# The opening of an attention and mixture-of-experts layer: the first tile's halves and product in front of the second tile's statistics and the weight scaling

## The chip, the cores and the metric

The kernel runs on one core of one Trainium2 chip. The metric is the device time of one execution in microseconds (us), the median of several runs. Five engines work beside each other, each through its own list of instructions in order: TensorE (PE, with its weight loads PEld), VectorE (DVE), ScalarE (ACT), GpSimd (POOL) and SyncE (SP), which here only issues DMAs. They meet by semaphores.

## The reference

The layer takes x of 8 x 512 x 256 in float32 and computes

```
x = x + attention(layernorm(x))          # q, k, v products of 256x256, causal softmax, scores / 16
x = x + ffn(layernorm(x))                # shared expert + 8 routed experts, 2 of them per token
ffn: down(silu(x gate) * (x up)), I = 512, weights of the two best sigmoid(router logits), normalised
layernorm(x) = (x - mean) / sqrt(var + 1e-5)
```

Queries and keys come in only as x Wq Wk^T x^T, so the kernel multiplies Wq and Wk^T once (wm) and needs one product t = x wm instead of two.

## The kernel before, in words

Everything that TensorE multiplies is split into two float16 parts, a high half (ScalarE copies the float32 value into float16) and a low half (the float32 value less the high half, in float16), and each product is three matmuls: high by high, high by low, low by high. So each operand passes ScalarE (names ending in `_high`) and then VectorE or GpSimd (`_low`).

The work is tiled by batch: eight tiles of 512 tokens, tile b in four blocks of 128 tokens. For each tile: statistics on VectorE (`stats_1`, line 1498, `aggregate_1`, whose last instruction writes ve, line 1490), the power -0.5 on GpSimd (`rstd1`, line 706), the shift on VectorE (`shift_1`, line 1509, writes nmr), the normalised tile on ScalarE (`xn_normalise`, line 962), its high half on ScalarE (`xn_high`, 975) and low half on GpSimd (`xn_low`, 712), a transposing DMA on SyncE's queue (`xn_transpose`, 386), then on TensorE the products t and v (`t_product`, 2333, `v_product`, 2353), their high halves on ScalarE (`t_high`, 1009, `v_high`, 1019) and low halves on VectorE (`t_low`, 1690, `v_low`, 1700), the scores, the row maxima, exp, the transposed probabilities and their product with v.

Tile 0 goes another way, so that it need not wait for a DMA: TensorE transposes it with an identity matrix (`first_transposes`, 2222), ScalarE and VectorE take the halves from PSUM (`first_xn_high`, 1087, `first_xn_low`, 1540). Two of its four blocks are normalised on VectorE.

The weights of the experts come in 36 pieces through two buffers: a load, `w_scale` (945) and `w_high` (951) on ScalarE, `w_low` (730) on GpSimd, which frees the buffer for the load two pieces on. wm, wv and the router's matrix are split at the start (`wm_low`, `wv_low`, `router_low`).

The order of the work is written out by hand: each engine has one list of calls, and an instruction whose semaphore isn't there holds back all that stands behind it on its engine. GpSimd's list begins rstd1(0), rstd1(1), the zeroing of the rows in DRAM (a DMA that it issues), rstd1(2), xn_low(1), w_low(0), put_idx(0), w_low(1), xn_low(2) (lines 785 to 793). Four waits matter near the change: `t_product(0)` waits for both low halves of tile 0 and for wm_low, `v_product(0)` for wv_low too, `t_high(0, ...)` for wv_low, whose source lies in the tensor that t_high writes, and `shift_1(2)` for rstd1(2) and for tile 1 to be normalised.

Of the kernel before, what the change touches and what calls it, by code (L numbers as in the profile page):

```python
# [91 lines left out]
def wait(eng, sem, value):  # L92

    if isinstance(value, int) and value <= 0:
        return
    eng.wait_ge(sem, value)
# [22 lines left out]
def build(nc, x, wq_t, wk_t, wv, w_all, router, bias, out):  # L119
    with ExitStack() as ctx:  # L120
# [212 lines left out]
        def bank3(o):  # L333
            return o[:, :].rearrange("p (n r) -> p n r", r=P)
# [22 lines left out]
        def blk(t3):  # L357
            return t3.rearrange("p (n d) -> p n d", n=NB)

        def w_ap(j, part, off, n):  # L360
            at_ = part * WJ + off
            if isinstance(j, int):
                return w[:, j * (2 * WJ) + at_:j * (2 * WJ) + at_ + n]
            return w[:, :].bitcast(U8)[:, ds(j * (4 * WJ) + 2 * at_, 2 * n)].bitcast(F16)
# [574 lines left out]
        def _(act):  # L939
            a = nc.scalar  # L940

            def copy(o, i, scale=1.0):
                return a.activation(o, i, ACT.Copy, scale=scale)  # L943

            def w_scale(g):

                piece = wst[:, (g % 2) * CH:(g % 2 + 1) * CH]
                act.wait_ge(w_in[g % 2], 16 * (g // 2 + 1))
                copy(piece, piece, WS).then_inc(w_scaled, 1)

            def w_high(g):

                j, c = divmod(g, CHUNKS)
                act.wait_ge(w_scaled, g + 1)
                if g == E * CHUNKS:
                    act.wait_ge(gu_mm, 4 * (B - 3) + 4)
                    act.wait_ge(xn2_lo, 2 * B - 2)
                    act.wait_ge(pt_in[1], 16 * B)
                    act.wait_ge(ln1, B * LN_STEPS)
                copy(w_ap(j, 0, c * CH, CH), wst[:, (g % 2) * CH:(g % 2 + 1) * CH]).then_inc(w_hi, 1)  # L960

            def xn_normalise(b):

                if b >= B:
                    return
                act.wait_ge(shift1, b + 1)
                if b == 1:
                    act.wait_ge(xn0_mm, 2)
                wait(act, xn_lo, b - 1)
                for i in range(2 if b == 0 else NB):  # L970
                    ins = a.activation(xn32[:, i * D:(i + 1) * D], x1[:, ds(b * (NB * D) + i * D, D)],
                                       ACT.Identity, scale=rstd[0][:, i:i + 1], bias=nmr[:, i:i + 1])
                ins.then_inc(xn_put, 1)

            def xn_high(b):

                if b >= B:
                    return
                act.wait_ge(xn_put, b + 1)
                wait(act, xnt_in, 16 * b - 16)  # L980
                copy(xnrow[:, :].rearrange("p (n c) -> p n c", n=NB)[:, :, 0:D], blk(xn32[:, :])).then_inc(xn_hi, 1)
# [27 lines left out]
            def t_high(b, m):  # L1009

                if b >= B:
                    return
                act.wait_ge(t_mm, b * KD + (m + 1))
                if b == 0:
                    act.wait_ge(wv_lo, 1)
                wait(act, s_mm, b * NB)
                copy(tt[:, m * S:(m + 1) * S], T_BANK[m][:, :]).then_inc(t_hi, 1)

            def v_high(b, m):

                if b >= B:
                    return
                act.wait_ge(v_mm, 2 * b + m + 1)
                wait(act, pv_mm, 2 * b)
                copy(v[:, m * S:(m + 1) * S], V_BANK[m][:, :]).then_inc(v_hi, 1)
# [61 lines left out]
            def first_xn_high(k):  # L1087

                act.wait_ge(xn0_mm, 2)
                copy(xnt4[:, :, k, :], bank3(XN_BANK[k])).then_inc(xn0_hi, 1)  # L1090
# [6 lines left out]
            def router_high():  # L1097

                act.wait_ge(small_in, 32)
                copy(rw[:, 0:KD * E], tt[:, 1024:1024 + 2 * KD * E].bitcast(F32), WS).then_inc(rw_hi, 1)  # L1100
# [7 lines left out]
            wv_high()  # L1108
            wm_high()
            router_high()  # L1110
            w_scale(0)
            first_xn_high(1)
            first_xn_high(0)
            xn_normalise(1)
            w_scale(1)
            xn_high(1)
            w_high(0)
            t_high(0, 0)
            w_high(1)
            t_high(0, 1)  # L1120
            v_high(0, 0)
            xn_normalise(2)
            exp_of(0, 0)
# [336 lines left out]
        def _(dve):  # L1460
# [6 lines left out]
            def low(o, full, hi, scale=None):  # L1467

                if scale is None:
                    return d.tensor_tensor(o, full, hi, ALU.subtract)  # L1470
                return d.scalar_tensor_tensor(out=o, in0=full, scalar=scale, in1=hi, op0=ALU.mult, op1=ALU.subtract)
# [4 lines left out]
            def stats_of(b, lns, tile):  # L1476

                for n in range(NB):
                    ins = d.bn_stats(tile[:, 6 * n:6 * n + 6], x_of(b)(n))
                ins.then_inc(lns, 1)  # L1480

            def aggregate(b, i, lns, shifted, tile):

                done = b * LN_STEPS
                dve.wait_ge(lns, done + 1)
                wait(dve, shifted, b)
                for n in range(NB):
                    d.bn_aggr(mv[i][:, 2 * n:2 * n + 2], tile[:, 6 * n:6 * n + 6]).then_inc(lns, 1)
                dve.wait_ge(lns, done + 5)
                d.tensor_scalar(ve[i][:, :], mv[i][:, :].rearrange("p (n c) -> p n c", c=2)[:, :, 1],  # L1490
                                EPS, None, ALU.add).then_inc(lns, 1)
# [6 lines left out]
            def stats_1(b):  # L1498

                if b < B:  # L1500
                    dve.wait_ge(x_in[b], 16)
                    stats_of(b, ln1, stats1)

            def aggregate_1(b):

                if b < B:
                    aggregate(b, 0, ln1, shift1, stats1)
# [32 lines left out]
            def first_xn_low(k):  # L1540

                dve.wait_ge(xn0_hi, k + 1)
                low(xnt4[:, :, KD + k, :], bank3(XN_BANK[k]), xnt4[:, :, k, :]).then_inc(xn0_lo, 1)

            def wv_low():

                dve.wait_ge(wv_hi, 1)
                low(wvs[:, KD * D:2 * KD * D], tt[:, 0:1024].bitcast(F32), wvs[:, 0:KD * D], WS).then_inc(wv_lo, 1)

            def router_low():  # L1550

                dve.wait_ge(rw_hi, 1)
                low(rw[:, KD * E:2 * KD * E], tt[:, 1024:1024 + 2 * KD * E].bitcast(F32), rw[:, 0:KD * E],
                    WS).then_inc(rw_lo, 1)

            def wm_low():

                dve.wait_ge(wm_hi, 1)
                low(wm[:, KD * D:2 * KD * D], PT0[:, :], wm[:, 0:KD * D], WS).then_inc(wm_lo, 1)
# [294 lines left out]
            first_xn_normalise()  # L1854
            stats_1(1)
            aggregate_1(1)
            stats_1(2)
            wm_low()
            shift_1(1)
            first_xn_low(1)  # L1860
            first_xn_low(0)
            router_low()
            aggregate_1(2)
            wv_low()
            stats_1(3)
            shift_1(2)
            t_low(0, 0)
# [902 lines left out]
```

## Time and profile before

| | |
|---|---|
| median of 3 runs | 556.28 us (555.76 to 557.24) |
| span of the profiled execution, first to last instruction | 555.3 us |
| median less that span | 0.98 us |
| PE busy | 518.0 us, 93% |
| DVE busy | 369.8 us, 67% |
| ACT busy | 301.0 us, 54% |
| POOL busy | 288.9 us, 52% |

No time beside its span is given for the profiled execution itself; the difference to the median is what this table shows. A row of a timeline has the start in us from the span's start, the length in us, the engine, the line of the kernel (a helper's line may stand for many calls), the operation, what it writes and reads with the shapes, and in brackets how long the engine was idle before and what ended that. Lengths of neighbours overlap by some 0.1 us.

### The profile page before, as it was taken

To read this page: it belongs to the slowest core of one execution; us is meant where nothing else is said; L and a number is where in the kernel's file an instruction comes from. 1 tells how busy PE (TensorE), PEld (TensorE's weight loads), DVE (VectorE), ACT (ScalarE), POOL (GpSimd) and SP (SyncE) were. 2 spreads that over 40 slices of the span, in tenths; PEclk is the share of its full clock that TensorE was granted. 3 is DMA by queue.
4 is the path that set the end of the run, shared out by engine and by line. 5 is a ranking of instruction groups with operands and counts; after the bars stand their busy time and mean duration, and the time that the engine had idled before them with its cause. 6 is when DMAs were issued, how large, how long until landed. Compare 5 with 4: busy or idle time off the path is not lost.

```text
span 555.3 us, 14903 instructions
## 1 busy us (share of the span) xinstructions
PE 518.0 (93%) x4757; PEld 425.5 (77%) x4757; DVE 369.8 (67%) x980; ACT 301.0 (54%) x580; POOL 288.9 (52%) x242
## 2 busy tenths in 40 slices
PE   4889988999999999997999999999999999999992
PEld 3557766788878888886767788888787888888881
DVE  5788998689887878899747555445454454454551
ACT  3989877678777676744233443433343433434341
POOL 4466677668676765857022344452444434434443
PEclk9999999899999999998899999999999999999998
DMA  8799848949694947414465965764846536345443
GB/s 271 201 181 208 178 127 158 217 133 209 161 208 141 194 127 170 155 70 136 131 115 85 98 107 69 103 83 60 108 59 89 73 60 97 55 65 78 62 58 38
DMA packets 139351, 68.55 MB, mean 123 GB/s; under 512 B 114608, under 2 KB 132336, under 8 KB 139280
## 3 DMA queue, kind: packets, MB, share of 16 engines
q1 hardware_dynamic: 126128, 48.84, 43.5%
q0 software_dynamic: 13152, 18.76, 19.4%
q8 instruction: 44, 0.72, 0.5%
q14 instruction: 27, 0.22, 0.1%
HBM read 19.46 MB, written 23.08 MB: 77 GB/s over the span
## 4 chain that ended last, share of the span: by engine, by line
PE 65%; DVE 12%; DMA 8%; SPq 5%; ACT 5%; issue 3%; POOL 1%; POOLq 0%; ACTq 0%; DVEq 0%
PE bank L2216 29%; PE bank L2240 15%; PE bank L2547 4%; PE bank L2322 3%; PE bank L2564 3%; DMA v<-xnrow 2%; PE bank L2625 2%; PE bank L2347 2%; PE bank L2392 2%; DMA xn2t<-xrow 2%; PE bank L2369 2%; PE bank L2640 2%; SPq L405 2%; DMA x<-x 1%; DVE h L1470 1%
## 5 line engine op out<-in xcount | busy, mean ns | idle before, releaser
L2216 PE MATMUL bank<-xn2t,w 128*128 128x256 f16 x1608 | 184.9, 273 | 1.3 <-DVE th L1653 1.1
L2216 PEld LDWEIGHTS bank<-xn2t,w 128*128 (+1 forms) x1608 | 155.2, 98 | 24.3 <-DVE th L1653 2.2
L1644 DVE SCALAR_TENSOR_TENSOR th<-th,bank 128x512 f32<-128x512 f32 x83 | 56.6, 682 | 55.2 <-ACT th L989 54.1
L2240 PE MATMUL bank<-w,h 128*128 (+1 forms) x768 | 91.5, 273 | 0.0
L943 ACT ACTIVATE h<-th 128x512 f16<-128x512 f32 (+1 forms) x69 | 42.9, 622 | 84.6 <-DVE th L1653 78.3
L989 ACT ACTIVATE th<-bank 128x512 f32<-128x512 f32 x83 | 49.2, 593 | 62.1 <-PE bank L2216 47.6
L2240 PEld LDWEIGHTS bank<-w,h 128*128 128x128 f16 x768 | 74.0, 98 | 10.4 <-DVE x L1676 0.3
L866 POOL DMA_INDIRECT out<-p,wm x28 | 43.9, 1569 | 67.2 <-ACT p L1323 27.3
L1470 DVE TENSOR_TENSOR h<-th,h 128x512 f16<-128x512 f32 (+1 forms) x69 | 50.6, 733 | 38.3 <-ACT h L943 38.1
L734 POOL TENSOR_TENSOR w<-wst,w 128x768 f16<-128x768 f32 x36 | 59.1, 1645 | 18.9 <-ACT w L943 18.7
L758 POOL DMA_INDIRECT rows<-xrow,sidx x56 | 56.5, 1009 | 17.0 <-issue 13.3
L866 POOL DMA_INDIRECT out<-phl,wm x24 | 38.1, 1587 | 39.1 <-DMA out<-tt,wm 13.0
L1653 DVE SCALAR_TENSOR_TENSOR th<-th,bank 128x512 f32<-128x512 f32 x83 | 56.8, 684 | 2.0
L866 POOL DMA_INDIRECT out<-tt,wm x12 | 19.7, 1644 | 41.0 <-DMA out<-x 17.2
L2216 PE MATMUL bank<-w 128*128 128x256 f16 x288 | 34.5, 280 | 0.0
L2547 PE MATMUL bank<-w,ptr 128*128 x144 | 33.0, 379 | 0.4 <-DMA ptr<-rows 0.4
L943 ACT ACTIVATE xnrow<-xn 128x512 f16<-128x512 f32 (+2 forms) x26 | 17.8, 684 | 26.1 <-DVE xn L2107 17.4
L2216 PEld LDWEIGHTS bank<-w 128*128 128x128 f16 x288 | 28.4, 100 | 4.2
L2322 PE MATMUL bank<-v,ptr 128*128 128x256 f16 x240 | 29.7, 273 | 1.2 <-DMA ptr<-phl 1.0
L943 ACT ACTIVATE wst<-wst 128x768 f32<-128x768 f32 x36 | 30.1, 836 | 0.6 <-DMA wst<-w_all 0.6
L943 ACT ACTIVATE w<-wst 128x768 f16<-128x768 f32 x36 | 30.1, 840 | 0.5
L704 POOL TENSOR_TENSOR rstd<-ve,halves 128x4 f32<-128x4 f32 x16 | 16.9, 1058 | 25.5 <-DVE ve L1490 23.0
(188 smaller groups left out, 808.4 us busy)
## 6 DMA issues: line engine op xcount, KB each, us to landing
wst<-w_all SPq DMA_DIRECT2D x36, 384.0 KB
x<-x SPq DMA_DIRECT2D x8, 512.0 KB, 5.6
out<-x SPq DMA_DIRECT2D x8, 512.0 KB, 4.0
rows<-xrow POOLq DMA_DIRECT2D x1, 1192.5 KB, 6.6
rows<-xrow,sidx POOLq DMA_INDIRECT x56
out<-p,wm POOLq DMA_INDIRECT x28
xn2t<-rows SPq DMA_TRANSPOSE x26
wm<-rows SPq DMA_DIRECT2D x26, 9.0 KB, 2.4
```

The costliest lines, as they stand in the source:

```text
L734: cc.tensor_tensor(w_ap(j, 1, c * CH, CH), wst[:, (g % 2) * CH:(g % 2 + 1) * CH], w_ap(j, 0, c * CH, CH), ALU.subtract).then_inc(w_lo, 1)
L758: cc.indirect_dma_start(rows, bass.IndirectOffsetOnAxis(ap=sidx_of(b)[:, m:m + 1], axis=0), xrow[b % 2][:, n * RW:(n + 1) * RW].bitcast(I3 ...
L866: cc.indirect_dma_start(out, bass.IndirectOffsetOnAxis(ap=index, axis=0), part, None, compute_op=ALU.add).then_inc(y_out, 16)
L943: return a.activation(o, i, ACT.Copy, scale=scale)
L989: a.activation(th[:, half * 512:(half + 1) * 512], G[half][:, :], ACT.Tanh, scale=0.5 / WS).then_inc(f_tanh, 1)
L1470: return d.tensor_tensor(o, full, hi, ALU.subtract)
L1644: d.scalar_tensor_tensor(out=tb, in0=tb, scalar=1.0, in1=G[half][:, :], op0=ALU.add, op1=ALU.mult).then_inc(f_sg, 1)
L1653: d.scalar_tensor_tensor(out=tb, in0=tb, scalar=0.5 / (WS * WS), in1=U[half][:, :], op0=ALU.mult, op1=ALU.mult).then_inc(f_h, 1)
L2216: ins = mm(dst, w_ap(j, ws, m * MAT + k * I + (2 * half + i) * P, P), moving(ms * KD + k), start=(cnt == 0), stop=(cnt == 3 * KD - 1))
L2240: ins = mm(o[:, a * D:(a + 1) * D], hb[:, (hs * KI + i) * TT + a * P:(hs * KI + i) * TT + (a + 1) * P], w_ap(j, ws, 2 * MAT + i * D, D), s ...
L2322: ins = mm(PV_BANK[q // 2][:, (q % 2) * D:(q % 2 + 1) * D], ptr[:, off + (ps * (q + 1) + kb) * P:off + (ps * (q + 1) + kb + 1) * P], v[:, ...
L2547: ins = mm(o[:, :], xs_t[:, c * P:(c + 1) * P], w_ap(j, ws, m * MAT + kk * I, I), start=(cnt == 0), stop=(cnt == 3 * KD - 1))
```

## The change

Two of the hand-written lists change their order; no instruction is added, removed or resized. On ScalarE, w_scale(0) goes behind the two high halves of tile 0, and the two t_high of tile 0 go in front of w_high(0) and w_high(1). On VectorE, stats_1(2) goes from in front of wm_low to behind router_low, and wv_low from behind aggregate_1(2) to in front of router_low.

```diff
@@ ScalarE's list @@
             router_high()
-            w_scale(0)
             first_xn_high(1)
             first_xn_high(0)
+            w_scale(0)
             xn_normalise(1)
             w_scale(1)
             xn_high(1)
+            t_high(0, 0)
+            t_high(0, 1)
             w_high(0)
-            t_high(0, 0)
             w_high(1)
-            t_high(0, 1)
             v_high(0, 0)
@@ VectorE's list @@
             aggregate_1(1)
-            stats_1(2)
             wm_low()
             shift_1(1)
             first_xn_low(1)
             first_xn_low(0)
+            wv_low()
             router_low()
+            stats_1(2)
             aggregate_1(2)
-            wv_low()
             stats_1(3)
```

## Rows read from the trace of the kernel before

**Rows 1.** Window: busy us (and instructions) of PE, PEld, DVE, ACT, POOL; clock, DMA.
```profile
14.30:31.00 16.70, 14.88 (x105) 9.59 (x106) 12.65 (x39) 16.57 (x34) 9.75 (x8) 1.00 0.85 210
```
**Rows 2.** Timeline of ScalarE from 12 to 26 us.
```profile
12.29 1.08 ACT L943 ACTIVATE xnt<-bank 128x512 f16<-128x512 f32 x2 [0.68 <-PE bank L2227]
14.33 2.07 ACT L971 ACTIVATE xn<-x,nmr,rstd 128x256 f32<-128x256 f32 x4 [0.96 <-DVE nmr L1495]
...
17.05 1.04 ACT L943 ACTIVATE xnrow<-xn 128x1024 f16<-128x1024 f32 x1
17.99 0.83 ACT L943 ACTIVATE w<-wst 128x768 f16<-128x768 f32 x1
18.73 0.57 ACT L943 ACTIVATE tt<-bank 128x512 f16<-128x512 f32 x1
...
19.94 0.57 ACT L943 ACTIVATE tt<-bank 128x512 f16<-128x512 f32 x1
...
20.89 2.07 ACT L971 ACTIVATE xn<-x,nmr,rstd 128x256 f32<-128x256 f32 x4
22.86 0.32 ACT L1033 ACTIVATE bank<-bank,nm 128x128 f32<-128x128 f32 x1
...
25.95 0.66 ACT L1033 ACTIVATE bank<-bank,nm 128x512 f32<-128x512 f32 x1
```
**Rows 3.** Timeline of VectorE from 9 to 25 us.
```profile
9.72 1.41 DVE L1479 BATCH_NORM_STATS2 w<-x 128x6 f32<-128x256 f32 x4 [0.78 <-DMA x<-x]
...
11.57 0.17 DVE L1490 TENSOR_SCALAR ve<-mv 128x4 f32<-128x4 f32 x1
...
14.21 1.28 DVE L1470 TENSOR_TENSOR xnt<-bank,xnt 128x512 f16<-128x512 f32 x2
15.41 0.16 DVE L1471 SCALAR_TENSOR_TENSOR rw<-tt,rw 128x16 f16<-128x16 f32 x1
...
15.98 0.69 DVE L1471 SCALAR_TENSOR_TENSOR wvs<-tt,wvs 128x512 f16<-128x512 f32 x1
16.58 1.40 DVE L1479 BATCH_NORM_STATS2 w<-x 128x6 f32<-128x256 f32 x4
17.90 0.15 DVE L1495 SCALAR_TENSOR_TENSOR nmr<-mv,rstd 128x4 f32<-128x4 f32 x1
...
20.55 0.69 DVE L1470 TENSOR_TENSOR tt<-bank,tt 128x512 f16<-128x512 f32 x1 [0.52 <-ACT tt L943]
...
24.99 0.69 DVE L1711 TENSOR_REDUCE mx<-bank 128x1 f32<-128x512 f32 x1
```
**Rows 4.** Timeline of TensorE from 15 to 26 us.
```profile
15.55 2.76 PE L2347 MATMUL bank<-xnt,wm 128*128 128x512 f16 x12 [3.30 <-DVE xnt L1470]
...
21.29 0.51 PE L2392 MATMUL bank<-xnt,tt 128*128 128x128 f16 x6 [0.35 <-DVE tt L1470]
...
25.09 1.46 PE L2347 MATMUL bank<-w,wm 128*128 128x512 f16 x6
```
**Rows 5.** Timelines of GpSimd and of SyncE's queue from 11 to 21 us.
```profile
11.82 1.01 POOL L704 TENSOR_TENSOR rstd<-ve,halves 128x4 f32<-128x4 f32 x1 [3.85 <-DVE ve L1490]
12.79 1.30 POOL L766 DMA_DIRECT2D rows<-xrow  x1
...
18.16 2.13 POOL L717 TENSOR_TENSOR xnrow<-xn,xnrow 128x1024 f16<-128x1024 f32 x1 [0.57 <-ACT xnrow L943]
...
20.32 2.23 SPq L393 DMA_TRANSPOSE w<-xnrow  x1
```
**Rows 6.** Timelines of VectorE and GpSimd where both work, at 41 and 103 us.
```profile
40.30 1.66 POOL L734 TENSOR_TENSOR w<-wst,w 128x768 f16<-128x768 f32 x1
41.25 0.72 DVE L1495 SCALAR_TENSOR_TENSOR nmr<-mv,rstd 128x4 f32<-128x4 f32 x1
...
103.13 0.97 POOL L758 DMA_INDIRECT rows<-xrow,sidx  x1 [0.30 <-issue]
103.42 0.23 DVE L1595 TENSOR_TENSOR one_hot<-eidx,idxf 128x64 f32<-128x64 f32 x1
```

## The prediction

> **What bounds the kernel now.** I read the page's busy shares first (TensorE 93% of the span), then the windows of the opening, then each engine's timeline up to 45 us, because the edit touches only two order lists and both lie ahead of 21 us. TensorE sets the pace of most of the kernel, but not of the opening. Between 14.30 and 31.00 us ScalarE is busy 16.57 of 16.70 us and TensorE 14.88 [rows 1]. ScalarE is idle twice before that, 0.68 us until the transposes of tile 0 are there and 0.96 us until tile 1's shift is there (nmr), and then works without a gap [rows 2]. TensorE waits 3.30 us for VectorE's low halves of tile 0 before its first product at 15.55, and starts the scores at 21.29, right behind VectorE's second t_low, 20.55 + 0.69 [rows 3, 4]. GpSimd makes tile 2's rstd, then xn_low(1) from 18.16 to 20.29, and SyncE transposes tile 1 at 20.32; the first product of tile 1 starts at 25.09 [rows 4, 5]. So the reader is to see three strands that meet at 25 us: ScalarE's chain, GpSimd and the transpose, and VectorE with TensorE. A lead of one is worth what the others allow.
>
> **VectorE's list.** Moved: stats_1(2) from before wm_low to behind first_xn_low, and wv_low ahead of it. Nothing is added. The old order: ve(1) starts at 11.57. The next, wm_low, can follow 0.08 later, at 11.65, and is over by 12.33 (a 128x512 split with scale takes 0.69, as wv_low does). shift_1(1) then waits for GpSimd's rstd(1), 11.82 + 1.01 = 12.83, and starts at 12.87. The first high half of tile 0 on ScalarE (two in 1.08 from 12.29, some 0.60 for the first) is there at 12.90, the second at 13.37. So the low halves start at 12.93 and 13.53 and end at 14.21, and TensorE's first product starts at 14.27 instead of 15.55: a lead of 1.28 us [rows 2 to 5]. That is all that the edit can give the product; the loads it is moved past are no part of it.
>
> The price: wv_low at 14.13, router_low at 14.74, stats_1(2) at 14.83, and ve(2) 1.85 us behind it (9.72 to 11.57), 16.68 to 16.85. stats_1(3) starts at 16.76 and leaves the engine at 18.08 (16.58 to 17.90 is 1.32), where shift_1(2) stands next in order [rows 3].
>
> **GpSimd.** rstd(2) stands ahead of xn_low(1) in its queue. It needs ve(2), so it starts at 16.93 (0.08 behind, as 11.74 to 11.82) and takes 1.0; xn_low(1) starts at 17.91 and ends at 20.04, SyncE's transpose starts at 20.07. ScalarE's high half ends at 17.77 (below), so it doesn't bind. This strand gains 0.25 us on 18.16 [rows 2, 5]. The four loads and transposes behind it on SyncE's queue move with it.
>
> **ScalarE's list.** w_scale(0) moved behind the two first_xn_high saves nothing in front of them: they waited 0.68 us for TensorE anyway. It now fills part of the 0.96 us wait: it starts at 12.29 + 0.98 = 13.27, and xn_normalise(1) follows 0.74 us later, as t_high behind a 768-wide copy does (17.99 to 18.73), at 14.01 (the shift was there at 13.02) instead of 14.33, a lead of 0.32 us. t_high(0,0) and t_high(0,1) stand in front of w_high(0) and w_high(1): they start at 17.99 - 0.32 = 17.67 and, 0.48 behind as the two in 1.08 at 12.29 stand, at 18.15, instead of 18.73 and 19.94. Their matmuls are over by 17.03 (14.27 + 2.76), and wv_low by 14.82. The high halves end at 18.24 and 18.72. The same instructions stand between xn_normalise(1) and xn_normalise(2), so that one is at 20.57, exp_of(0,0) could be at 22.54 instead of 22.86 [rows 2, 4]. w_high(0) ends at 19.46, w_high(1) at 20.2, ahead of xn_low(1)'s end, so GpSimd's w_low and the weight loads lose nothing.
>
> **What is late next.** VectorE could take t_low(0,0) at 18.28. But shift_1(2), a 128x4 operation with both inputs in SBUF, stands in front of it, ready at 18.08, and GpSimd has been in xn_low(1) since 17.91. What that does is in the trace: the same shift at 41.25 took 0.72 us instead of 0.15 and ended at 41.97, when GpSimd's w_low (40.30 + 1.66) ended at 41.96 [rows 3, 6]. So I let shift_1(2) hang until 20.05, with both t_low behind it: t_low(0,0) at 20.0, t_low(0,1) at 20.6 to 21.29, scores at 21.34 instead of 21.29. In the order of before the shift ran at 17.90, ahead of xn_low(1) at 18.16 [rows 3, 5]. The lead of 1.28 us at the product is gone, by a lock that this order meets and the old one missed by 0.26 us.
>
> By the Trainium skill (SBUF — State Buffer, Who interferes with whom) a VectorE instruction with two SBUF inputs contends with a GpSimd instruction that reads SBUF, whichever starts first holds the shared port for its whole length, and one with a PSUM input and an SBUF input doesn't contend. The row at 41.25 agrees. By the rule the sum is the one of this paragraph; without it scores would start 1.6 us earlier, and the sum would be that of rival one.
>
> From there: the last scores of tile 0 end 0.05 later than before, so row_max(0,3), which began at 24.99 right behind them, begins at 25.04, takes 0.69, and its minus some 0.18 more (a small operation's 0.15 and the pass between), which is 25.91; exp_of(0,3), at 25.95 before, starts at 25.93. ScalarE's 0.32 us is used up there [rows 2, 3]. TensorE's product of tile 1 needs the scores out of the way and the transpose: 25.1 against 25.09. GpSimd's and SyncE's 0.25 us stays only in the transposes of p, whose landing TensorE reaches while it is nearly busy. **Sum:** between 0 and -0.25 us, and I take -0.1, because two of the three strands come out at zero. All of it against the profiled execution's span of 555.3; the median lies 0.98 us above that span, which holds what is outside it, so I carry the difference over to 556.28. Forecast 556.2 us.
>
> **What the trace of before doesn't show.** shift_1(1) would now run at 12.87, inside GpSimd's issue of the zero rows (12.79 to 14.09), where before no operation with two SBUF inputs stood. Bounds: 0, as one_hot at 103.42 took its 0.23 us beside an indirect DMA's issue of 103.13 to 104.10, and 1.22 us, to the end of the issue at 14.09 [rows 5, 6]. A gain is excluded, it can only wait. I take 0, the row that is nearest in kind. The loads that wst and tiles 2 and 3 need had landed by 16.6 at the latest (stats_1(3) ran then without idle time); stats_1(2) comes 2.6 us later than before, and w_scale(1) 0.3 earlier, bounded between 0 and 0.3 us of wait.
>
> **Rivals.**
> One: shift_1(2) isn't held, because GpSimd starts xn_low(1) after 18.08 or the lock spares it. Then t_low starts at 18.28, the scores at 19.7 (behind the v products), 1.6 us earlier, and the strands that bound are ScalarE (-0.32) and the transpose (-0.25): 556.0. For it: the margin is only 0.17 us. Against it: VectorE's and GpSimd's times both hang on ve(2), so the margin doesn't drift.
>
> Two: the whole lead at the product reaches the end, -1.28 to -1.6: 554.8. For it, TensorE is the busiest engine. Against it, ScalarE has 0.13 us of idle time in 16.7 us, and no work is taken from it [rows 1].
>
> Three, slower: the issue of the zero rows holds the same port, and shift_1(1) hangs until 14.1. The low halves of tile 0 end at 15.3, the product is at 15.4, stats_1(2) at 15.95, ve(2) ends at 17.97, xn_low(1) runs from 19.03 to 21.16, shift_1(2) ends with it, and the scores start at 22.45, 1.16 us late; the exps of tile 0, row_max(0,3) above all, follow: 557.4. It decides as soon as shift_1(1) lasts more than some 0.1 us. The skill's same section, on which operations grab the pair, infers that descriptor generation needs the write interface, while two inputs take only the read interface; by that this rival costs nothing.
>
> That the edit doesn't do what it says is excluded for the product, but half true for ScalarE: scaling the weights wasn't what the high halves waited for.
>
> **How the numbers follow.** Forecast 0.60, rival one 0.17, rival three 0.10, rival two 0.06, and 0.07 for a shift of the later waits either way: GpSimd's locks fall on other VectorE operations too, and a hit costs up to 2 us. A measurement of this kernel tells about 0.3%, 1.7 us, from no change. The forecast and rivals one and three are inside that; rival two is at its edge. So faster 0.06, same 0.88, slower 0.06. The range holds the forecast and rivals one and three with 0.5 us for a median (three runs were 555.76 to 557.24): 555.3 to 557.4.
>
> **What would show it.** In the changed trace: the first product at 14.3; xn_normalise(1) at 14.0; t_high(0,0) at 17.7; xn_low(1) at 17.9; shift_1(2) lasting 2 us and ending with xn_low(1); scores at 21.3; the product of tile 1 at 25.1. A shift_1(1) of over 1 us is rival three, a shift_1(2) of 0.15 us with scores at 19.7 is rival one. The forecast is wrong if the 21 to 31 us stretch moves by over 0.5 us, or if a difference arises only after it.

## The result: 560.05 us in the first comparison, no difference in four more

In the first comparison the changed kernel took 560.05 us (median of 5 runs, 557.90 to 562.46) against 556.28 us for the old one (5 runs, 555.57 to 557.24): ratio 1.007, 95% interval 1.0041 to 1.0100. That is outside my range of 555.3 to 557.4. Four more comparisons, on four different chips, did not bring the difference back. Each had 12 runs of the changed kernel and 23 to 35 of the old one:

| comparison | changed: median (lowest to highest) | old: median (lowest to highest) | ratio, 95% interval |
|---|---|---|---|
| first | 560.05 (557.90 to 562.46), 5 runs | 556.28 (555.57 to 557.24), 5 runs | 1.0070, 1.0041 to 1.0100 |
| again | 558.83 (555.86 to 565.30) | 559.45 (554.21 to 564.06) | 0.9995, 0.9966 to 1.0024 |
| again2 | 560.97 (557.26 to 567.33) | 562.39 (556.86 to 567.06) | 0.9997, 0.9961 to 1.0032 |
| again3 | 557.62 (553.66 to 558.26) | 556.31 (552.75 to 561.87) | 0.9997, 0.9966 to 1.0029 |
| again4 | 559.51 (554.49 to 564.62) | 560.70 (557.86 to 566.31) | 0.9963, 0.9933 to 0.9993 |

The medians and their ranges are over all runs; the ratio leaves out runs more than 1.5% above the fastest of their kernel, and so can stand up to 0.3% from the ratio of the two medians. In each of the four later comparisons the old kernel's own runs lie 8 to 10 us apart, in the first one 1.7 us. Its median differs by 6 us from chip to chip.

**The opening, after.** The order of events came out as the steps say. VectorE's timeline of the changed kernel from 11 to 22 us answers to [rows 3]:

```profile
11.44 0.17 DVE L1490 TENSOR_SCALAR ve<-mv 128x4 f32<-128x4 f32 x1
11.52 0.68 DVE L1471 SCALAR_TENSOR_TENSOR wm<-bank,wm 128x512 f16<-128x512 f32 x1
12.73 0.16 DVE L1495 SCALAR_TENSOR_TENSOR nmr<-mv,rstd 128x4 f32<-128x4 f32 x1 [0.54 <-POOL rstd L704]
12.81 1.28 DVE L1470 TENSOR_TENSOR xnt<-bank,xnt 128x512 f16<-128x512 f32 x2
...
16.55 0.17 DVE L1490 TENSOR_SCALAR ve<-mv 128x4 f32<-128x4 f32 x1
16.62 1.40 DVE L1479 BATCH_NORM_STATS2 w<-x 128x6 f32<-128x256 f32 x4
17.94 2.03 DVE L1495 SCALAR_TENSOR_TENSOR nmr<-mv,rstd 128x4 f32<-128x4 f32 x1
19.89 1.27 DVE L1470 TENSOR_TENSOR tt<-bank,tt 128x512 f16<-128x512 f32 x2
```

The row to look at is 17.94: the 128x4 shift of tile 2, 0.15 us before, takes 2.03 and ends at 19.97. GpSimd's timeline shows the holder, which ends at 19.94:

```profile
11.69 1.01 POOL L704 TENSOR_TENSOR rstd<-ve,halves 128x4 f32<-128x4 f32 x1 [3.61 <-DVE ve L1490]
12.65 1.30 POOL L766 DMA_DIRECT2D rows<-xrow  x1
16.81 1.03 POOL L704 TENSOR_TENSOR rstd<-ve,halves 128x4 f32<-128x4 f32 x1 [2.86 <-DVE ve L1490]
17.82 2.12 POOL L717 TENSOR_TENSOR xnrow<-xn,xnrow 128x1024 f16<-128x1024 f32 x1
```

TensorE, against [rows 4]: the first product 1.40 us earlier, the scores 0.07, tile 1's product 0.30.

```profile
14.15 2.76 PE L2347 MATMUL bank<-xnt,wm 128*128 128x512 f16 x12 [2.56 <-DVE xnt L1470]
16.75 2.78 PE L2369 MATMUL bank<-wvs,xnt 128*128 128x256 f16 x24
21.22 0.51 PE L2392 MATMUL bank<-xnt,tt 128*128 128x128 f16 x6 [1.68 <-DVE tt L1470]
...
24.79 1.46 PE L2347 MATMUL bank<-w,wm 128*128 128x512 f16 x6
```

ScalarE, against [rows 2]: xn_normalise(1) is 0.99 us ahead, xn_normalise(2) 0.85, and at exp_of(0,3) 0.12 is left of it.

```profile
11.63 1.08 ACT L943 ACTIVATE xnt<-bank 128x512 f16<-128x512 f32 x2 [1.08 <-PE bank L2227]
12.61 0.84 ACT L943 ACTIVATE wst<-wst 128x768 f32<-128x768 f32 x1
13.34 2.07 ACT L971 ACTIVATE xn<-x,nmr,rstd 128x256 f32<-128x256 f32 x4
...
20.04 2.08 ACT L971 ACTIVATE xn<-x,nmr,rstd 128x256 f32<-128x256 f32 x4
22.34 0.34 ACT L1033 ACTIVATE bank<-bank,nm 128x128 f32<-128x128 f32 x1 [0.22 <-DVE nm L1718]
...
25.83 0.66 ACT L1033 ACTIVATE bank<-bank,nm 128x512 f32<-128x512 f32 x1
```

**The rest of the run.** The profiled execution took 557.90 us with a span of 556.2, 0.9 over the span of before; it was the fastest of the five, whose slowest had a span of 560.6. So no one trace holds the 3.8 us between the medians. Windows of the changed kernel (columns as in [rows 1]):

```profile
66.00:74.00 8.00, 6.44 (x57) 3.86 (x56) 6.79 (x27) 7.19 (x14) 4.74 (x6) 0.80 0.96 196
96.00:102.00 6.00, 4.32 (x44) 3.34 (x45) 4.04 (x12) 2.61 (x5) 3.86 (x5) 0.72 1.01 199
256.00:268.00 12.00, 7.01 (x64) 5.81 (x62) 11.14 (x36) 4.95 (x8) 5.16 (x4) 1.00 0.34 87
```

and the same windows of the old kernel:

```profile
66.00:74.00 8.00, 7.89 (x86) 6.32 (x85) 7.79 (x28) 7.94 (x16) 4.73 (x6) 1.00 0.87 173
96.00:102.00 6.00, 4.04 (x45) 3.26 (x46) 3.77 (x10) 2.57 (x5) 3.56 (x5) 0.79 0.97 198
256.00:268.00 12.00, 8.86 (x56) 6.55 (x55) 11.32 (x35) 5.01 (x7) 5.79 (x5) 0.72 0.40 110
```

The column to read is the granted clock. A value under 1.00 means that for part of the window TensorE had 1.2 GHz instead of 2.4. The two traces have such parts in different places: the changed one at 66 to 74 us, behind a wait of 1.45 us for a transpose, the old one at 256 to 268, behind a wait of 3.14. A wait alone doesn't decide it: the changed trace has the same wait, 3.15 us in front of its row at 260.15, and full clock behind it. The 24 matmuls there took 2.79 us, in the old trace 5.30:

```profile
260.15 2.79 PE L2240 MATMUL bank<-w,p 128*128 128x256 f16 x24 [3.15 <-DVE x L1676]
```

```profile
261.10 5.30 PE L2240 MATMUL bank<-w,p 128*128 128x256 f16 x24 [3.14 <-DVE x L1676]
```

The other piece is a landing. Just ahead of it the changed trace is 0.82 us in front (305.45 against 306.27). Then a product of the singles (the smaller blocks of routed tokens) starts 0.91 us later than in the old trace, behind 2.32 us of wait for its DMA where the old one waited 0.58. So the two traces shift by 1.73 us against each other at this one place. The changed kernel:

```profile
305.45 2.78 PE L2216 MATMUL bank<-xn2t,w 128*128 128x256 f16 x24
310.55 1.47 PE L2564 MATMUL bank<-w,v 128*128 x12 [2.32 <-DMA v<-xnrow]
```

and the old one:

```profile
306.27 2.78 PE L2216 MATMUL bank<-xn2t,w 128*128 128x256 f16 x24
309.64 1.48 PE L2564 MATMUL bank<-w,v 128*128 x12 [0.58 <-DMA v<-xnrow]
```

From there to the end the changed trace stays 0.9 to 1.1 us behind. None of these places is touched by the edit.

### The profile page after: what moved, and what is told of

It is laid out like the page before. It is cut to its first block, busy times and chain, and to the rows that moved or that the text cites. A ratio compares the mean times of both kernels' runs of the same rounds, so it can differ in the third digit from the quotient of the medians.

```text
span 556.2 us, 14903 instructions
## 1 busy us (share of the span) xinstructions
PE 515.8 (93%) x4757; PEld 424.3 (76%) x4757; DVE 369.6 (66%) x980; ACT 301.7 (54%) x580; POOL 292.2 (53%) x242
## 3 DMA queue, kind: packets, MB, share of 16 engines
q0 software_dynamic: 13152, 18.76, 19.6%
## 4 chain that ended last, share of the span: by engine, by line
PE 67%; DVE 9%; DMA 7%; SPq 6%; issue 3%; POOL 3%; ACT 3%; POOLq 0%; ACTq 0%; DVEq 0%
PE bank L2216 30%; PE bank L2240 15%; PE bank L2547 4%; PE bank L2392 3%; PE bank L2322 3%; PE bank L2564 3%; DMA v<-xnrow 3%; PE bank L2347 2%; PE bank L2625 2%; PE bank L2369 2%; PE bank L2640 2%; SPq L405 1%; DVE h L1470 1%; DVE th L1653 1%; DMA w<-xrow 1%
## 5 line engine op out<-in xcount | busy, mean ns | idle before, releaser
L758 POOL DMA_INDIRECT rows<-xrow,sidx x56 | 59.0, 1054 | 16.9 <-issue 13.3
L866 POOL DMA_INDIRECT out<-tt,wm x12 | 19.8, 1652 | 41.4 <-DMA out<-x 17.4
```

The source lines that it names most:

```text
L758: cc.indirect_dma_start(rows, bass.IndirectOffsetOnAxis(ap=sidx_of(b)[:, m:m + 1], axis=0), xrow[b % 2][:, n * RW:(n + 1) * RW].bitcast(I3 ...
L866: cc.indirect_dma_start(out, bass.IndirectOffsetOnAxis(ap=index, axis=0), part, None, compute_op=ALU.add).then_inc(y_out, 16)
```

## Experiments

Theory W: the two orders cost the same; single executions wander by several us with half-clock stretches and landings, and the first comparison drew an unlike set. Theory C: the change costs some 0.7%, by its VectorE list (the hold) or by its ScalarE list. The ratio and interval of each are against the old kernel's runs beside it.

**again: the changed kernel, unaltered.**

> The changed kernel once more, unaltered. Its first profile shows an opening 0.1 to 0.3 us ahead of the old one at 25 us, and a loss of 0.9 us that arises at 300 to 310 us; single runs went from 557.9 to 562.5. Theory C (the change does cost time, by something that comes later than the opening): median 559 to 561, every run above the old kernel's. Theory W (it costs nothing, and the runs fell on late landings and on half-clock stretches by chance): median 556 to 557.5, runs of both kernels mixed.

0.9995 (0.9966 to 1.0024). Theory C's 1.004 and more is outside the interval.

**act_only: only ScalarE's part of the diff.**

```diff
-            w_scale(0)
             first_xn_high(1)
             first_xn_high(0)
+            w_scale(0)
...
+            t_high(0, 0)
+            t_high(0, 1)
             w_high(0)
-            t_high(0, 0)
             w_high(1)
-            t_high(0, 1)
```

> Only ScalarE's list is changed. Opening: the first product stays at 15.5, VectorE's shift of tile 2 is not held by GpSimd (0.15 us), t_high of tile 0 is about 1 us earlier, scores at some 20.3. Theory C by ScalarE's list: 559 to 561. Theory C by VectorE's list, or theory W: 555.5 to 557.

1.0035 (1.0000 to 1.0070), median 561.05: between the theories, undecided alone. The shift of tile 2 wasn't held (0.14 us). The scores started at 22.36 and not at 20.3. A half-clock stretch fell on the first product, whose 12 matmuls took 4.36 us instead of 2.76. Even at full clock 20.3 was out of reach: the v products stand in front of the scores, and in the trace of before they end at 20.94 (18.16 + 2.78). TensorE's timeline:

```profile
15.55 4.36 PE L2347 MATMUL bank<-xnt,wm 128*128 128x512 f16 x12 [2.72 <-DVE xnt L1470]
19.75 2.78 PE L2369 MATMUL bank<-wvs,xnt 128*128 128x256 f16 x24
22.36 0.50 PE L2392 MATMUL bank<-xnt,tt 128*128 128x128 f16 x6
```

**dve_only: only VectorE's part.**

```diff
-            stats_1(2)
             wm_low()
...
+            wv_low()
             router_low()
+            stats_1(2)
             aggregate_1(2)
-            wv_low()
```

> Only VectorE's list is changed. The first product is 1.2 us earlier, and the shift of tile 2 is held by GpSimd's low half of tile 1 for about 2 us; scores at 21.3 or later. Theory C by VectorE's list (the hold): 559 to 561. Theory C by ScalarE's list, or theory W: 555.5 to 557.5.

1.0019 (0.9989 to 1.0048), median 559.84. The hold is there (2.02 us), the first product at 14.62, the scores at 21.67; this profile's span was 554.0, the shortest of all profiles. So the hold alone doesn't make a run long. VectorE's timeline:

```profile
18.40 2.02 DVE L1495 SCALAR_TENSOR_TENSOR nmr<-mv,rstd 128x4 f32<-128x4 f32 x1
20.34 1.27 DVE L1470 TENSOR_TENSOR tt<-bank,tt 128x512 f16<-128x512 f32 x2
```

**shift_late: the changed kernel without the hold in front of t_low.**

```diff
-            shift_1(2)
             t_low(0, 0)
             t_low(0, 1)
+            shift_1(2)
```

> The changed kernel, with tile 2's shift behind both low halves of t, so that GpSimd's hold (still about 0.5 us or more of it) no longer stands in front of them. Scores of tile 0 at 19.6 instead of 21.2, the product of tile 1 still at 24.8, as it waits for the transpose of tile 1. If the hold on VectorE costs the 4 us: 555.5 to 556.5. If it is something else: 559 to 561, with the scores 1.6 us earlier all the same.

1.0000 (0.9968 to 1.0032), median 559.87. The shift was held for 0.46 us only, and t_low(0,0) ran at 19.20, inside GpSimd's operation of 19.08 to 21.20, in its usual 0.67 us: here the operation with one PSUM and one SBUF input was not held, and the one with two SBUF inputs was, from 20.77 to 21.23. Tile 1's statistics started 1.13 us later than in the trace of before and a half-clock stretch hit the first product, so the scores stood at 21.95, and my 19.6 was not seen. Counted from the start of tile 1's statistics they came after 11.10 us, where the changed kernel's first trace has 11.63 with the hold in it (21.22 - 9.59). In the whole time no gain and no loss shows. VectorE's rows, then GpSimd's:

```profile
17.89 1.40 DVE L1479 BATCH_NORM_STATS2 w<-x 128x6 f32<-128x256 f32 x4
19.20 0.67 DVE L1470 TENSOR_TENSOR tt<-bank,tt 128x512 f16<-128x512 f32 x1
20.16 0.69 DVE L1470 TENSOR_TENSOR tt<-bank,tt 128x512 f16<-128x512 f32 x1 [0.29 <-ACT tt L943]
20.77 0.46 DVE L1495 SCALAR_TENSOR_TENSOR nmr<-mv,rstd 128x4 f32<-128x4 f32 x1
```

```profile
19.08 2.12 POOL L717 TENSOR_TENSOR xnrow<-xn,xnrow 128x1024 f16<-128x1024 f32 x1
```

**base_again and base_again2: the old kernel against itself.**

> The old kernel against itself: what a comparison of this size makes of no change. Theory W (single executions wander by 2 to 3 us with the half-clock stretches and the landings that they hit, so that five runs against five can differ by 0.7% with nothing changed): 0.997 to 1.003 with twelve runs, single times from 554 to 564, and profiles of it that differ by whole half-clock stretches. If runs of one kernel agreed within 0.3%, theory W would fall.

> The old kernel against itself on that occasion: the size of a difference that means nothing. 0.997 to 1.003, and its profile's opening within 1.5 us of the other openings of the old kernel, moved by when tile 1 of x lands.

0.9996 (0.9958 to 1.0034), medians 561.76 and 562.39, single runs from 556.71 to 567.06; and 0.9999 (0.9967 to 1.0031), 561.68 and 560.70. With nothing changed, 12 runs against 23 to 35 leave an interval of 0.3 to 0.4% each way. And the old kernel's opening isn't fixed: its profile in base_again2 started tile 1's statistics at 11.62 instead of 9.72, because x landed later, and had its first product at 17.4, at a clock of 0.72 from 12 to 24 us:

```profile
11.62 1.41 DVE L1479 BATCH_NORM_STATS2 w<-x 128x6 f32<-128x256 f32 x4 [2.44 <-DMA x<-x]
```

```profile
12.00:24.00 12.00, 7.83 (x33) 4.12 (x33) 8.68 (x31) 8.11 (x13) 7.27 (x7) 0.72 0.52 176
```

I had expected the openings within 1.5 us of each other; this one was 1.90 us behind that of the first trace and 2.14 behind that of base_again, and its scores stood at 25.30, 4.0 us behind those of before.

The longest profiled execution, that of base_again (span 564.3), had an opening like the first trace's: its scores started at 21.09. Of its 9.0 us over that trace 6.85 had arisen by the product of the singles, at 316.49 instead of 309.64. A late opening isn't what made this one long.

```profile
316.49 1.52 PE L2564 MATMUL bank<-w,v 128*128 x12 [2.50 <-DMA v<-xnrow]
```

**again2, again3, again4: the changed kernel on three more chips.**

> The changed kernel a third time, to have more runs of it. Theory W: 0.997 to 1.003. Theory C (the change costs 0.7%, and the last comparison missed it by chance): 1.004 to 1.010.

> The changed kernel once more. Theory W: 0.997 to 1.003 of the old kernel, single times spread over 8 us or more. A chip on which the first comparison's 1.007 comes back (old kernel's runs within 2 us of each other, the changed one's above) would speak for theory C on that chip.

> The changed kernel on a further occasion. If the scatter of 8 us or more is the rule (theory W): 0.997 to 1.003, old kernel's runs 8 us apart. If there are occasions on which the old kernel keeps within 2 us and the changed one lies above: 1.004 to 1.010 here or in none of four.

0.9997, 0.9997 and 0.9963 (the table). The last is outside what I expected, and on the other side. No occasion brought back old runs within 2 us of each other.

**fill_before and fill_after: TensorE kept busy in three waits.** The added matmuls compute nothing that is used.

```diff
+            def fill(n):
+                for _ in range(n):
+                    mm(Y[:, :].rearrange("p (n r) -> p n r", r=P), ident[:, :],
+                       maskb[:, :].unsqueeze(1).to_broadcast([P, NB, P]), start=True, stop=True)
...  # fill(12) in the old order, fill(8) in the new, ahead of t_product(0)'s waits;
...  # fill(8) ahead of xn2_ready(2) in logits(2); fill(8) in shared_down(13) behind its y_read wait
```

> The old order with TensorE kept busy in the three waits that half-clock stretches followed in the profiles (12 matmuls of 512 columns ahead of the first product, 8 ahead of the third tile's logits, 8 ahead of the fourteenth shared down product; their results are overwritten or never read). If the half-clock stretches that begin in these waits make the scatter and some of the level: no such stretch but the one at the end, mean clock 0.991 or more, median 1 to 3 us under the old kernel's, the slowest runs gone. If the scatter comes from landings of DMAs alone: clock up, but median and scatter as before, within 1 us.

> The same filling in the changed kernel (8 matmuls ahead of the first product, whose wait is shorter). With the clock held, the two orders can be told apart better: theory W and my forecast say within 0.5 us of the filled old kernel; theory C says 3 to 4 us above it.

1.0029 (0.9995 to 1.0064), median 562.63, and 1.0032 (0.9991 to 1.0072), 562.38. The two orders stand 0.25 us apart, as theory W says; theory C's 3 to 4 us is outside the uncertainty of that difference, some 1.7 us each way (an estimate from the two standard deviations, 1.9 and 2.2 us, of 12 runs each). Of the two branches for fill_before the second came out: the mean clock over the runs rose from 0.987 to 0.990 and 0.991, and both medians stayed within 0.3 us of the old kernel's 562.39. The gain of 1 to 3 us, had the half-clock stretches set the level, didn't come. What the added matmuls themselves cost wasn't measured apart. In fill_after the filling left 0.77 us of the wait in the opening, and the first product ran at full clock, in 2.76 us. In fill_before the filling ended at 14.21, TensorE waited 2.71 us more for VectorE's low halves, late with x's tiles (tile 1's statistics began at 11.13), and the half-clock stretch came all the same: the first product took 4.11 us.

```profile
11.46 2.75 PE L2190 MATMUL bank<-maskb,ident 128*128 128x512 bf16 x12
16.93 4.11 PE L2356 MATMUL bank<-xnt,wm 128*128 128x512 f16 x12 [2.71 <-DVE xnt L1470]
```

**bias_early and both: another hold taken away.** VectorE's three copies of the biases, 128x8, stood at 32.41 and took 1.81 us beside GpSimd's low halves of weights, with the maxima of tile 1 behind them. The old kernel's rows, VectorE's and GpSimd's:

```profile
32.41 1.81 DVE L1565 COPY biases<-biases 128x8 f32<-128x8 f32 x3
```

```profile
30.82 3.24 POOL L734 TENSOR_TENSOR w<-wst,w 128x768 f16<-128x768 f32 x2
```

```diff
             router_low()
+            bias_rows()
...
-            bias_rows()
```

`both` is this edit in shift_late.

> The old kernel with the three small copies of the biases right behind router_low alone. Same expectation: exp of tile 1 begins at 32.7 to 33 instead of 34.3; 0.997 to 0.998 of the old kernel if it lasts to the end, 1.000 if not.

> The changed kernel with tile 2's shift behind both t_low (no hold in front of the scores) and with VectorE's three small copies of the biases right behind router_low, at 14.8, where GpSimd is idle, instead of at 32.4, where GpSimd's low halves of weights hold them for 1.6 us with the scores of tile 1 behind them. If such a hold is paid on the way to the end: 1 to 1.7 us less than the old kernel, 0.997 to 0.998. If waits further on take it up, as they took the lead of the first product: 1.000.

The copies took 0.31 us in their new place, at 17.33 in bias_early, and ScalarE's wait in front of tile 1's first exp fell from 2.12 us to 0.96 (bias_early) and 0.26 (both). The time didn't move: 1.0005 (0.9968 to 1.0042) and 1.0012 (0.9975 to 1.0048), medians 556.98 and 558.76 against 556.31. Beside the trace of before, whose scores started at 21.29, both profiles opened late (scores at 24.50 and 22.93), so the 32.7 to 33 us expected for the first exp of tile 1 wasn't seen: it stood at 36.31 in bias_early and at 34.53 in `both`. TensorE's product of tile 2 in bias_early still waited 1.72 us for VectorE at 44, where the old trace has 1.53 at 40.9; whether a gain of a microsecond in one engine's wait is absorbed there, or is only too small for this comparison, isn't shown. Neither is a version that beats the old kernel measurably.

```profile
17.33 0.31 DVE L1565 COPY biases<-biases 128x8 f32<-128x8 f32 x3
```

## Why the prediction was wrong, step by step

- **The product's lead, 1.28 us:** right; 1.40 in the first profile. The extra 0.12 lies ahead of the edit: tile 1's ve was at 11.44 instead of 11.57.
- **ve(2) at 16.68, xn_low(1) at 17.91, the shift ready at 18.08 and held until 20.05, scores at 21.34:** right; 16.55, 17.82, 17.94 to 19.97, 21.22, in each case 0.1 earlier. The hold is the same in all profiles with this VectorE order (2.02 or 2.03 us), as the margin between xn_low(1) and the shift doesn't depend on when x lands. By the Trainium skill (SBUF — State Buffer, Who interferes with whom) a VectorE operation with two SBUF inputs contends with a GpSimd operation that reads SBUF, and one with at most one SBUF input doesn't, outside VectorE's 2-port modes. shift_late agrees with both halves, 0.46 us of hold and a free 0.67. A single input alone is no safeguard: the copies of the biases, one SBUF input each, took 1.81 us at 32.41 and 0.31 at 17.33.
- **ScalarE's lead, 0.32 us:** 0.99 at xn_normalise(1) and 0.85 at xn_normalise(2). Mis-sized, as the transposes of tile 0 ended earlier (tile 0's high halves began at 11.63 instead of 12.29): their 16 matmuls took 1.95 us, and 2.40 in the trace of before; the other profiles have 1.95 to 3.17. At exp_of(0,3) 0.12 was left, where I said 0.02.
- **Tile 1's product, 25.1:** mis-sized; it started at 24.79, 0.30 us earlier than before. I had it bound by the scores. In the trace of before it had also waited for the DMA that transposes tile 1, and that DMA started 0.35 us earlier (19.97 instead of 20.32), where I had 0.25. So this strand came out at 0.30 at TensorE, and not at zero.
- **shift_1(1) beside the zero rows' issue, taken at 0:** right; 0.16 us at 12.73, inside the issue of 12.65 to 13.95. Rival three is out.
- **Rival one and rival two:** the hold came, and of the product's lead of 1.40 us 0.07 was left at the scores. A gain of the 1.28 us that rival two needs lies outside one of the two intervals of the next point and inside the other.
- **The sum, 0 to -0.25 us:** the four large comparisons, weighted by their intervals, give 0.9987 (0.9972 to 1.0003), -0.7 us with -1.6 to +0.2. By the plain means over all runs it is -0.2 us (-1.0 to +0.5). The sum is inside both; a gain or loss of a few tenths isn't told apart from it.
- **The median less the span, 0.98 us:** mis-read. I took it for what lies outside the span. In all 283 runs that have both numbers the time is 1.68 to 1.87 us over the span, so the trace of before came from an execution of about 557.0 us, some 0.7 or 0.8 above the median. That doesn't touch the forecast difference, but it was a sign that single executions differ.
- **The step that failed** is the one that turned the sum into a range: "The range holds the forecast and rivals one and three with 0.5 us for a median (three runs were 555.76 to 557.24)", and with it "A measurement of this kernel tells about 0.3%, 1.7 us, from no change". Three runs that happened to lie 1.5 us apart were taken for the kernel's scatter. In 122 further runs of the old kernel the standard deviation of a single run within one comparison is 2.0 to 2.6 us. If I draw two sets of five from the old kernel's runs of one comparison, returning each run before the next draw, their medians differ by the 3.77 us of the first comparison or more in 1 to 8% of the draws. Without returning them it is 2, 7 and 3% on three chips and under 0.1% on the fourth. So no term of the sum is shown to be wrong by 3.8 us; what failed is the width put on a median.
- **What the scatter goes with:** in part the clock. The mean clock of a run, times its span, gives the time at half clock, 11 to 15 us on average (twice the missing share of the clock, times the span); in the profiles 5 to 8 us of it lie at the end, where TensorE is idle. Over the old kernel's runs each us of it goes with 0.70, 0.63, 0.31 and 0.15 us of time on the four chips (correlation 0.78, 0.64, 0.48, 0.23). The profiles put stretches at 14 to 23, 71 to 74, 98 to 104, 249 to 267 and, in base_again, 318 to 321 us, each in or behind a wait of TensorE of 1.45 to 4.98 us, in some executions and not in others of one kernel. Waits of that length also pass at full clock: 3.30 us at 15.55 in the trace of before, 3.15 at 260.15 in the changed one. That the stretches cause the scatter isn't shown: the filling raised the clock and not the speed. The landing of x (tile 1's statistics from 9.48 to 11.63) and of the single rows at 310 us (0.41 to 2.50 us of wait) are the other part that the profiles show.

**Open:** whether the first comparison was only a chance draw. Five old runs within 1.7 us came up in 1 to 9% of draws from the later sets, and both things together, such a narrow five and medians 3.77 us apart, in fewer than one draw in a thousand. 1.007 stands outside the intervals of all four others. Which chip it ran on isn't known, so a property of that chip or of that occasion can't be excluded: the scatter may have been smaller there and the difference real. Against it stand four chips without such a difference. The first two traces say little: behind 25 us I found no row that leads back to the edit, but the changed trace is of the fastest of five executions, and TensorE's distance between the two swings by more than a microsecond either way before 305 us.

## What to carry to other kernels

Take the scatter of a kernel from many executions before you put a range on a change of a few tenths of a percent: three runs told 1.5 us here where 23 to 35 told 8 to 10. A reordering that brings a product forward by a microsecond has to be followed to the place where the strands meet again, and there a small operation with two SBUF inputs that starts 0.12 us behind GpSimd's can give the whole lead away. Moving the three small copies to where GpSimd is idle took their hold away here (0.31 us instead of 1.81), but it moved no measurable time.

## What the runs showed of the hardware

- The 128x4 operation with two SBUF inputs was held for the rest of a 2.13 us GpSimd operation that began some 0.1 us before it, in seven profiles out of seven (2.02 or 2.03 us); started 0.26 us ahead of it in the trace of before, and 0.05 us ahead in bias_early, it took 0.15 and 0.14 us.
- Three 128x8 copies with one SBUF input each took 1.81 us beside GpSimd's operations of 30.82 to 34.06, and 0.31 us elsewhere.
- GpSimd's issue of a plain DMA (1.30 us) didn't hold it: 0.16 us.
- The same 12 matmuls of 512 columns took 2.76 us at full clock and 4.08 to 5.30 us with a stretch at half clock in them. The same wait in front, 3.14 or 3.15 us at 260 us, was followed by half clock in one trace and full clock in the other.
- Medians of one unchanged kernel on four chips: 556.31, 559.45, 560.70 and 562.39 us.
